# A drain of TensorE behind each pair of edge products, and a finished tile's first product cut in four, in a graph network's first edge sum

## What is computed

```python
x = x + L0_gnn(_layernorm(x), [src, dst], edge_weight)
# L0_gnn:
h = einsum('nd,df->nf', x, W)
agg = segment_sum(A_values[:, None] * h[col], row, num_segments=6250)
h = agg + bias                      # then batch norm over the nodes, relu
```

## Time and profile before

| | |
|---|---|
| runs (median) | 3917.03 us |
| profiled execution, span | 3891.6 us |
| first edge sum, first gather to barrier | 369.8 to 1558.8 us |
| second edge sum, for comparison | about 1950 to 3167 us |
| TensorE busy over the span | 2650.3 us (68%) |
| VectorE busy | 2586.9 us (66%) |
| GpSimd busy | 2179.1 us (56%) |
| ScalarE busy | 1024.1 us (26%) |
| mean granted TensorE clock | 0.819 of full speed |

### The profile page before, as it was taken

One profiled execution on the slowest core, in us unless ns is written; L12 is line 12 of the kernel. 1 busy time (PEld: TensorE's weight loads), 2 busy tenths in 40 slices (PEclk: granted clock), 3 DMA queues, 4 the chain that ended last, 5 costly groups with the idle time before them and its releaser, 6 DMA issues. The chain is left out here.

```text
span 3891.6 us, 55224 instructions
## 1 busy us (share of the span) xinstructions
PE 2650.3 (68%) x15016; PEld 2238.8 (58%) x15016; DVE 2586.9 (66%) x6599; ACT 1024.1 (26%) x2120; POOL 2179.1 (56%) x2145
## 2 busy tenths in 40 slices
PE   6886555444454545789946666666666657999998
PEld 4666343333343434689935444444444537999998
DVE  8997655444554555976746566666666677888886
ACT  0021000000000000567501111111111127888886
POOL 1434566666666664335456666666666603666665
PEclk8998777777777777899967777777887768999999
DMA  3011333333333332000133333333333334776775
GB/s 90 4 46 58 102 91 92 91 91 88 91 92 88 92 88 63 12 1 23 55 90 96 96 96 96 96 96 94 98 95 94 95 103 165 216 216 212 213 215 146
DMA packets 164219, 387.69 MB, mean 100 GB/s; under 512 B 46324, under 2 KB 95528, under 8 KB 150561
## 3 DMA queue, kind: packets, MB, share of 16 engines
q0 software_dynamic: 99072, 233.49, 22.0%
q1 hardware_dynamic: 64929, 151.65, 11.4%
HBM read 342.69 MB, written 42.97 MB: 99 GB/s over the span
## 5 line engine op out<-in xcount | busy, mean ns | idle before, releaser
L1089 POOL DMA_INDIRECT g_got<-table,e_source x1568 | 1493.5, 952 | 845.0 <-issue 440.0
L1115 DVE TENSOR_TENSOR A<-A,psum 128x256 f32 x1664 | 698.6, 420 | 876.3 <-remote 532.0
L1182 PE MATMUL psum<-g_got,g_route 128*128 x3328 | 1034.7, 473 | 141.0 <-DMA g_got<-table,e_source 74.2
L1182 PEld LDWEIGHTS psum<-g_got,g_route 128*128 128x128 f32 x3328 | 771.9, 241 | 329.0 <-issue 198.4
L786 PE MATMUL psum<-ident,g_rows 128*128 128x128 f32 x208 | 63.0, 401 | 663.3 <-ACT A L834 410.2
L1098 DVE TENSOR_SCALAR g_route<-columns,e_local,e_weight 128x128 f32<-128x128 f32 x1664 | 471.6, 362 | 17.4 <-issue 12.2
L786 PEld LDWEIGHTS psum<-ident,g_rows 128*128 128x128 f32 x208 | 29.7, 190 | 703.8 <-ACT A L834 505.7
L834 ACT COPY A<-psum 128x256 f32 x52 | 19.3, 372 | 999.4 <-issue 637.4
L369 POOL DMA_INDIRECT records<-rec,place x120 | 120.6, 1005 | 233.7 <-ACT rec L585 159.1
L140 PE MATMUL psum<-e_xt_hi,e_w_hi 128*128 128x256 f32 x832 | 238.2, 286 | 5.4 <-issue 5.2
L1612 POOL TENSOR_TENSOR f_ht_lo<-f_ht,f_ht_hi 128x512 fp32r<-128x512 f32 x100 | 134.2, 1347 | 181.1 <-ACT f_ht_hi L1551 174.6
(11 more groups left out here) (413 smaller groups left out, 5403.5 us busy)
## 6 DMA issues: line engine op xcount, KB each, us to landing
e_w<-in_m_w SPq DMA_DIRECT2D x104, 1024.0 KB, 5.1
g_got<-table,e_source POOLq DMA_INDIRECT x1568
expert_table<-g_normal SPq DMA_DIRECT2D x52, 128.0 KB
table<-xn SPq DMA_DIRECT2D x49, 128.0 KB
X<-in_x SPq DMA_DIRECT2D x1, 6144.0 KB
table<-f_ring SPq DMA_DIRECT2D x24, 256.0 KB, 2.1
out<-X SPq DMA_DIRECT2D x1, 6144.0 KB
f_w<-in_f_w SPq DMA_DIRECT2D x2, 1024.0 KB, 6.5
```

Source lines behind the costliest of these rows:

```text
L1089: pool.indirect_dma_start(got[:, c % RING, :], None, rows, bass.IndirectOffsetOnAxis(ap=source[:, c:c + 1].bitcast(U32), axis=0)).then_inc ...
L1115: dve.tensor_tensor(to, to, sums_of(c), ALU.add).then_inc(added, 1)
L1182: ins = pe.matmul(sums_of(c), route[:, c % (GB + GSEM), :], row(got, at[j % GSEM]), start=True, stop=True)
```

## The change

In the first edge sum alone, `pe.drain()` follows each pair of products, so TensorE's sequencer takes nothing further until its products have ended. The work on the finished tile is placed between pairs: `turn` behind the step's fourth pair (the same place as before), and `first_product` in four pieces of one product each, behind pairs five to eight. Piece 0 carries the waits, piece 3 the increment. Before, the four products stood together behind the sixth pair. At the end of the sum `turn` and `first_product` are called for the last tile as before, and the second edge sum keeps its order and gets no drain.

```diff
-            def first_product(self, pe, k):
-                pe.wait_ge(self.loaded, 16)
-                pe.wait_ge(self.xt_out, k + 1)
-                for b in range(KD):
-                    for i in range(KD):
-                        ins = pe.matmul(psum[:, 7, D + b * P:D + (b + 1) * P], self.w[:, i, b * P:(b + 1) * P],
-                                        self.xt[:, i, :], start=i == 0, stop=i == KD - 1)
-                ins.then_inc(self.across, 1)
+            def first_product(self, pe, k, pieces=range(KD * KD)):
+                for piece in pieces:
+                    if piece == 0:
+                        pe.wait_ge(self.loaded, 16)
+                        pe.wait_ge(self.xt_out, k + 1)
+                    b, i = divmod(piece, KD)
+                    ins = pe.matmul(psum[:, 7, D + b * P:D + (b + 1) * P], self.w[:, i, b * P:(b + 1) * P],
+                                    self.xt[:, i, :], start=i == 0, stop=i == KD - 1)
+                    if piece == KD * KD - 1:
+                        ins.then_inc(self.across, 1)
...
+                    def between_pairs(n, pair):
+
+                        if n >= 1 and pair == 3:
+                            tiles_of.turn(pe, n - 1)
+                        if n >= 1 and pair >= GB // 2 - KD * KD:
+                            tiles_of.first_product(pe, n - 1, (pair - (GB // 2 - KD * KD),))
+
...
                                 if c % 2 == 1:
                                     ins.then_inc(pairs_summed, 1)
+                                    if not through_mlp:
+                                        between_pairs(n, j // 2)
+                                        pe.drain()
...
-                            if n >= 1 and g == 1:
+                            if through_mlp and n >= 1 and g == 1:
                                 tiles_of.turn(pe, n - 1)
-                            if n >= 1 and g == (3 if through_mlp else 2):
+                            if through_mlp and n >= 1 and g == 3:
                                 tiles_of.first_product(pe, n - 1)
```

## The result

The change made the kernel slower: 3994.68 us (3981.60 to 4003.20, 4 runs) against 3915.34 us (3912.73 to 3925.56, 4 runs) for the kernel before, ratio 1.019 with a 95% interval of 1.0166 to 1.0214. Two later comparisons, both on one chip, gave 1.0222 (1.0188 to 1.0256) and 1.0240 (1.0194 to 1.0287). The profiled execution of the changed kernel has a span of 3979.8 us, with a mean granted clock of 0.80.

The account below looks back on a forecast made before the run. Bound: late increments and GpSimd's ring pauses, 23.3 us a long step. With 19.5 us steps, 51.1 remaining take 997 us from 418.6, plus 8.7: barrier 1424.3, gain 134.5, 3917.0 to 3783 us; range 3740 to 4040.

Parts of the forecast that it names:

- The circle: First sum: held increments would free GpSimd's ring, so 16 gathers, then 3.3 us pause; 23.3 us a long step.
- the arithmetic on GpSimd: First sum's floor: 783 gather steps at 1.25 us, 980 us, last gather at 1350, some 15 us more; 3723 us.
- the stayed hold: Rival, first sum: TensorE's increments stay held back because that depends on gathers, not density; 108 us lost, 4025 us, chance 0.34.
- go out pair by pair: First sum: with TensorE emptied behind each pair, pairs_summed increments would come promptly; late time entered at nothing.
- The prompt dense block of the earlier trace: Twelve dense products at 459.55, 5.35 us, releasing VectorE at once while GpSimd stood still for 16.41 us.
- 7.5 us of hold over an idle array: Evidence against: increments arrived 7.5 us after TensorE's array stopped, so idleness alone doesn't end the holding back.
- The cost of a drain: Behind each first-sum pair: 0.04 us after the product plus 0.13 restart, and lost overlap; 2.24 or 1.29 us a pair by clock.
- group head: Start of each group on TensorE: waiting for gathers and loading four places, now uncovered; 0.5 us a group, 2.0 a step.
- The step of 19.5 us: TensorE's first-sum step: a fifth of the work at full clock, 0.2 x 12.9 + 0.8 x 21.1 us.
- the rival's sum: If increments stay held: 4.7 + 21.1 = 25.8 us needed against 23.3 between releases, excess 2.4 in some 45 long steps.
- far above 4100: Time if each drain waited for a held increment, stopping TensorE until gathers run dry; a fifth of 0.34.
- The low clock: Rival, first sum: prompt increments but TensorE stays at 1.2 GHz, 21.1 us a step; 53 us gained, 3864 us, chance 0.16.

Follow-up runs that it names:

- plain_dmas_before: Plain DMAs from SyncE replace all first-sum gathers, no drains, pieces kept, against the same kernel with drains: barrier at 1126.1, against 1129.9.
- few_columns_before: The kernel before with 16 of 256 columns in each first-sum product behind the first 14 slots, no drains: 3953.50 us against 3917.80.
- group_drain: The changed kernel with 208 drains in place of 416, against the kernel before: 1.0000 on the chip without late completions, 1.0172 on a chip with them.
- plain_dmas_again: The changed kernel, drains kept, with plain DMAs from SyncE replacing all first-sum gathers, run on a chip with the kernel before at 3914 us: barrier at 1129.9.

## Why the prediction was wrong, point by point

- **What bounds the kernel.** The circle was read rightly: late increments, GpSimd's pauses at the ring's end, 171 us of waits. Without gathers or with plain DMAs it is gone, and the chip without holds ran the stage to 1372.8, near the 1365 that the arithmetic on GpSimd gave.
- **What it said, and what came.** The forecast was 3783 us, a gain of 134 us; measured were 3994.68 us, a loss of 79. The stated range of 3740 to 4040 holds that time only because it took in the stayed hold, which had a chance of 0.34.
- **The step that failed** is the expectation that the increments would "go out pair by pair", because "the drains must keep it from beginning"; the sum had the late time at zero. Measured were 102 late drains, 322 us, 6.2 us a step. The step rested on "dense stretches are what precedes each hold". The prompt dense block of the earlier trace rows spoke against density already, but there GpSimd stood still too. plain_dmas_before (dense, no gathers, no hold) and the changed kernel (broken up, with gathers, holds) told the two apart. The evidence against that I had written down beside it, 7.5 us of hold over an idle array, was the better guide.
- **The cost of a drain.** The 0.04 us behind the product measured 0.05, the restart of 0.13 measured 0.16 (from the drain's end to the next product), and the 0.5 us of a group head 0.49. The pairs at the lower clock stand as forecast, 2.24 us apart forecast, 2.28 measured (1104.30 to 1106.58), 2.77 over a group head (1106.58 to 1109.35):
```profile
1104.30 2.07 PE L1191 MATMUL psum<-g_got,g_route 128*128 x4 [0.92 <-issue]
1106.58 2.07 PE L1191 MATMUL psum<-g_got,g_route 128*128 x4 [0.21 <-issue]
1109.35 2.07 PE L1191 MATMUL psum<-g_got,g_route 128*128 x4 [0.70 <-DVE A L1117]
```
- **The step of 19.5 us.** Less its late drains (322 us in 52 steps, 6.2 us each) the step took 24.0 - 6.2 = 17.8 us. The clock was better than assumed: 0.71 is the full level for 42% of the time, not a fifth, and with 0.42 the forecast's own prices give 17.7. So TensorE by itself would have been just inside GpSimd's 18.9 us (an estimate: it takes the clock to be the same without the late drains). The error, 24.0 against 19.5, is the 6.2 us that the sum held at zero, less 1.7 for the clock. In the rival's sum 25.8 less 23.3 is 2.5 and not 2.4 us, which changes nothing.
- **The pieces and the queues.** The waits were costed at nothing, and TensorE's wait for `turn` is 3.3 us in 52 steps. The work that lengthens the segments was costed at 0.24 us a piece and 0.25 for the transposes; measured in the changed kernel are 0.31 and 0.29 on average (a piece ends 0.22 us behind its pair at the full clock and 0.43 at the lower one, as 856.95 + 2.07 to 858.81 + 0.64 above).
- **The rival that came true** is the hold that stays because it depends on the gathers, at 4025 us. In kind it was right, and its 108 us stand against 77 measured. But its working was of another thing: TensorE starting late after a release with a longer step. What happened is its last clause, that the drain itself waits, and there the price was wrong, "far above 4100". I took every drain to wait until the gathers run dry. Only a quarter of them met a hold, about two a step, and half of these ended while gathers still flowed. Also, a TensorE that has waited at its drains no longer waits for VectorE and ScalarE later: the 514 us before the transposes are gone. So much of the new waiting stands in the place of old waiting.
- **The rule of the Trainium skill** that I weighed (PSUM — Partial Sum Buffer, Engine vs sequencer instructions: increments attached to a matmul fire on its completion) would have a drain make nothing earlier and only cost. For the time this was the better guide. As a statement about when the increment is seen, the traces with holds differ from it by up to 7.5 us, and drains with an increment of their own end up to 9.6 us late; on the chip without holds the trace agrees (VectorE starts 0.14 us after the pair's end).
- **The low clock** as a rival of its own did not decide: the granted 0.71 is close to the 0.73 of before.

## What to carry over

If something comes late although the engine that makes it has long been idle, don't expect that emptying the engine more often brings it sooner: here a drain turned the late signal into a stop of the engine. Before forecasting a gain from breaking up a dense stretch, look for a stretch where the density is there and the other suspect is not; rows in which both change together prove neither. And look at what an experiment left in place: few_columns_before took away columns, not the dense stream. A wait that appears as "remote" or "issue" and whose length follows another engine's DMA issue is worth one run on a second chip.

## What the runs showed of the hardware

- Completions of TensorE, both increments on products and drains, are seen late while GpSimd issues indirect gathers in long runs: up to 9.0 and 11.9 us in the changed kernel, up to 15.4 with half the drains. Gathers of 16 rows do it as well as of 128; plain DMAs of 128 KB from SyncE at 140 GB/s do not; nor do gathers in fours with a wait for their landing between. Whether completions of other engines are held too was not looked at.
- It depends on the chip. Four groups of runs, on three chips, and the first comparison (its chip isn't on record) had the kernel before at 3902 to 3918 us; one chip had it at 3510 us, 10% less, with the same instruction durations (gather 954 ns there, 953 in the changed kernel). On that chip the profile also gives a time from issue to landing for the gathers, and in the profiles of all others none. From the tables of DMA issues, group_drain and then the changed kernel:
```profile
g_got<-table,e_source POOLq DMA_INDIRECT x1568, 2.8
```
```profile
g_got<-table,e_source POOLq DMA_INDIRECT x1568
```
  Why the chips differ, and by what way the gathers hold TensorE's completions back, no run shows. Whether the changed kernel gains or loses on the chip without holds wasn't tried; group_drain, at 1.0000, is the nearest.
- With few columns the clock fell to 0.51 over the stage although the time hardly moved. With plain DMAs in place of the gathers it was 0.98 with drains and 0.85 without, on the same chip (plain_dmas_again and plain_dmas_before); I had expected drains to lower it:
```profile
369.00:1129.00 760.00, 544.91 (x2243) 382.82 (x2241) 606.36 (x1788) 59.64 (x156) 0.00 (x0) 0.98 0.47 140
```
```profile
369.00:1125.00 756.00, 535.51 (x2243) 440.26 (x2241) 606.05 (x1788) 59.40 (x155) 0.00 (x0) 0.85 0.47 140
```
